# Graph attention layer: inverse sums and the shift's sign on POOL, output blocks finished in pairs

## What is computed

```python
h = relu(layernorm(x))                      # over the last axis, eps 1e-5
Wh = h @ W
f1, f2 = Wh @ a[:256, 0], Wh @ a[256:, 0]
e = f1[:, :, None] + f2[:, None, :]
e = where(e >= 0, e, 0.2 * e)
att = softmax(where(adj > 0, e, -9e15), axis=1)   # over i, for each column j
out = x + elu(einsum('bij,bjo->bio', att, Wh))
```

## Time and profile before

| | us |
|---|---|
| three runs | 1093.25, 1095.69, 1096.59; median 1095.69 |
| the profiled execution | 1092.74 |
| its span, from first to last instruction | 1091.0 |
| busy: PE, DVE, ACT, POOL | 972.8, 978.4, 958.3, 401.7 |
| first mask_scores begins | 61.9 |
| last mask_scores begins | 1049.8 |
| from one mask_scores to the next: middle of batch 7, middle of a batch 1 to 6 | 7.17 or 7.2, 7.3 to 8.7 |

### The profile page before, as it was taken

One profiled execution on the slowest core, in us unless ns is written; L12 is line 12 of the kernel. 1 busy time (PEld: TensorE's weight loads), 2 busy tenths in 40 slices (PEclk: granted clock), 3 DMA queues, 4 the chain that ended last, 5 costly groups with the idle time before them and its releaser, 6 DMA issues. The chain is left out here.

```text
span 1091.0 us, 24411 instructions
## 1 busy us (share of the span) xinstructions
PE 972.8 (89%) x8963; PEld 831.9 (76%) x8963; DVE 978.4 (90%) x1579; ACT 958.3 (88%) x1606; POOL 401.7 (37%) x317
## 2 busy tenths in 40 slices
PE   4667799899999999899998999999999999888987
PEld 3445688788878888787887888787887878777776
DVE  4379999999999999999999999999999999999973
ACT  3368999999999999998999999998999989988974
POOL 2313323334343433334343343334333343333334
PEclk9769999999999999999999999999999999999999
DMA  4366665666676676666766666766766566766614
GB/s 129 113 184 168 167 174 163 193 181 193 190 207 181 180 217 180 189 179 197 200 190 197 180 195 188 208 176 186 211 191 186 172 192 171 198 179 184 180 35 150
DMA packets 325654, 195.11 MB, mean 179 GB/s; under 512 B 9760, under 2 KB 321312, under 8 KB 325536
## 3 DMA queue, kind: packets, MB, share of 16 engines
q1 hardware_dynamic: 325536, 193.56, 62.2%
HBM read 176.69 MB, written 16.84 MB: 177 GB/s over the span
## 5 line engine op out<-in xcount | busy, mean ns | idle before, releaser
L689 POOL TENSOR_TENSOR direct<-prob,inv 128x1024 f16<-128x1024 f32 x128 | 242.6, 1895 | 590.7 <-DVE inv L605 585.2
L589 DVE CUSTOM_DVE_ANT_0 prob<-tp,f_row 128x2048 f32<-128x2048 bf16 x128 | 293.3, 2291 | 4.9 <-issue 4.4
L378 PE MATMUL acc<-v,direct 128*128 128x256 f16 x1024 | 280.2, 274 | 11.1 <-DVE direct L613 6.0
L360 PE MATMUL acc_st<-v,stored 128*128 128x256 f16 x992 | 270.2, 272 | 22.2 <-DVE z_st L629 21.6
L380 PE MATMUL acc<-v,direct 128*128 128x256 f16 x1024 | 279.9, 273 | 0.0
L382 PE MATMUL acc<-v,direct 128*128 128x256 f16 x1024 | 279.9, 273 | 0.0
L362 PE MATMUL acc_st<-v,stored 128*128 128x256 f16 x992 | 270.3, 272 | 0.0
L361 PE MATMUL acc_st<-v,stored 128*128 128x256 f16 x992 | 270.3, 272 | 0.0
L439 ACT ACTIVATE prob<-prob,shift 128x2048 f32<-128x2048 f32 x128 | 256.6, 2005 | 10.8 <-issue 0.4
L432 ACT ACTIVATE prob<-prob,f 128x2048 f32<-128x2048 f32 x128 | 255.6, 1997 | 0.0
L331 PEld LDWEIGHTS tp<-ident_b,neg 128*128 128x128 bf16 x2048 | 119.5, 98 | 94.1 <-issue 92.1
(11 more groups left out here) (71 smaller groups left out, 1222.4 us busy)
## 6 DMA issues: line engine op xcount, KB each, us to landing
raw<-in_adj SPq DMA_DIRECT2D x128, 1024.0 KB, 6.0
x_in<-in_x SPq DMA_DIRECT2D x128, 128.0 KB, 5.0
y<-in_x SPq DMA_DIRECT2D x128, 128.0 KB, 4.6
out<-y SPq DMA_DIRECT2D x128, 128.0 KB, 3.7
f_row<-f_scratch SPq DMA_DIRECT2D x32, 256.0 KB, 5.0
f_scratch<-f_t SPq DMA_DIRECT2D x128, 0.5 KB
w_cat<-in_W SPq DMA_DIRECT2D x1, 256.0 KB, 2.9
prob<-in_a SPq DMA_DIRECT2D x1, 256.0 KB, 3.7
```

Of the source, the lines that this page charges most:

```text
L360: nc.tensor.matmul(bank[:, 0:FO], p_st[:, 0, rows], v_c[:, 0, :], start=(c == 0), stop=False)
L378: nc.tensor.matmul(acc[:, m, :], p_d[:, 0, rows], v_c[:, 0, :], start=(j == 0 and m % 2 == 0), stop=False, skip_group_check=True)
L589: nc.vector.tensor_tensor_reduce(out=prob[:, c % 2, :], in0=tp_b, in1=f1_row[:, b % 2, :], scale=1.0, scalar=-3.0e38, op0=ALU.add, op1=ALU ...
L689: nc.gpsimd.tensor_tensor(direct[:, c % 2, 0, :], p[:, 0:HALF], k.to_broadcast([P, HALF]), ALU.mult).then_inc(hi_direct, 1)
```

## The change

POOL's `split_high(s)` first multiplies the sum by 2^-14 and raises it to the power -1 (column `minus_one`). ACT no longer negates the maximum: POOL's new `make_shift(s)` does, behind `split_high(s - 1)` and the additions of that step. DVE's `reciprocal` and `scale_inverse` are gone. Blocks are finished two at a time, 512 columns an instruction and 256 KB a transfer, in every second step. Buffers are changed to make room: one x buffer less, h_t single after the start. The diff, cut to its core:

```diff
-    RX = 7
+    RX = 6
-    RY = 8
-    RZ = 3
-    RE = 4
+    RY = 4
+    RZ = 4
+    RE = 2
...
-        h_t = sb("h_t", [P, 2, KC, P], F32)
+        h_t = sb("h_t", [P, KC, P], F32)
...
+        def h_buf(c):
+            return h_t_early if c < LEAD and c % 2 else h_t[:]
...
-        ORDER = {2: [0, 8], 3: [1], 4: [2], 5: [3, 9], 6: [4], 7: [5], 8: [6], 9: [7],
-                 10: [10], 11: [11], 12: [12], 13: [13], 14: [14], 15: [15]}
-        ORDER_LAST = {2 + q: [q, 8 + q] for q in range(8)}
+        ORDER = {2: [4], 3: [0], 5: [1], 7: [2], 9: [3], 11: [5], 13: [6], 15: [7]}
+        ORDER_LAST = {2: [4], 3: [0], 4: [5], 5: [1], 6: [6], 7: [2], 8: [7], 9: [3]}
...
-                if chunk(s + 25) and s + 25 >= RX:
-                    load_x(s + 25)
+                if chunk(s + 24) and s + 24 >= RX:
+                    load_x(s + 24)
...
+                wait(act, shift_s, c - R + 1)
                 nc.scalar.activation(most[:, c % R:c % R + 1], top[:, c % R:c % R + 1], ACT.Prelu, bias=f2, alpha=ALPHA
                                      ).then_inc(most_s, 1)
                 nc.scalar.activation(p, p, ACT.Prelu, bias=f2, alpha=ALPHA).then_inc(leaky, 1)
-                act.wait_ge(most_s, c + 1)
-                nc.scalar.activation(shift[:, c % R:c % R + 1], most[:, c % R:c % R + 1], ACT.Copy, scale=-1.0
-                                     ).then_inc(shift_s, 1)
                 act.wait_ge(leaky, c + 1)
                 act.wait_ge(shift_s, c + 1)
-                wait(act, recip_s, c - R + 1)
+                wait(act, total_s, c - R + 1)
...
-                if chunk(s):
-                    reciprocal(s)
-                    scale_inverse(s)
...
             def split_high(c):
                 p = prob[:, c % 2, :]
                 k = inv[:, c % R:c % R + 1]
+                t = small_total[:, c % R:c % R + 1]
+                pool.wait_ge(prob_ready, c + 1)
+                nc.gpsimd.tensor_scalar(t, total[:, c % R:c % R + 1], 2.0 ** -P_BITS, None, ALU.mult).then_inc(total_s, 1)
+                pool.wait_ge(total_s, c + 1)
+                wait(pool, lo_stored, c - R + 1)
+                nc.gpsimd.tensor_tensor(k, t, minus_one[:], ALU.pow).then_inc(inv_ready, 1)
                 pool.wait_ge(inv_ready, c + 1)
...
+            def make_shift(c):
+                pool.wait_ge(most_s, c + 1)
+                wait(pool, prob_ready, c - R + 1)
+                nc.gpsimd.tensor_scalar(shift[:, c % R:c % R + 1], most[:, c % R:c % R + 1], -1.0, None, ALU.mult
+                                        ).then_inc(shift_s, 1)
...
             for s in range(FIRST, END + 2):
                 if chunk(s - 1):
                     split_high(s - 1)
                 for k in finish(s - 2):
                     finish_add(k)
+                if chunk(s):
+                    make_shift(s)
```

More of the change, by code:

```diff
@@ L69, in graph_attention @@
         z_st = sb("z_st", [P, RZ, FO], F32)
-        elu = sb("elu", [P, RE, FO], F32)
+        elu = sb("elu", [P, RE, 2 * FO], F32)
         x_in = sb("x_in", [P, RX, F], F32)
-        y = sb("y", [P, RY, FO], F32)
+        y = sb("y", [P, RY, 2, FO], F32)
         xn = sb("xn", [P, 2, F], F32)
-        h_t = sb("h_t", [P, 2, KC, P], F32)
+        h_t = sb("h_t", [P, KC, P], F32)
         f12 = sb("f12", [P, 64 + RF], F32)
@@ L83, in graph_attention @@
         ones = prob[0:1, 0, 1024:1024 + P]
+        h_t_early = prob[:, 1, 1024:1024 + F].rearrange("p (k c) -> p k c", k=KC)
         w_nat = w_cat[:, :, 0:FO]
@@ L92, in graph_attention @@
         minus_half = sb("minus_half", [P, 4], F32)
+        minus_one = sb("minus_one", [P, 1], F32)
         top = sb("top", [P, R], F32)
@@ L96, in graph_attention @@
         total = sb("total", [P, R], F32)
-        inv_total = sb("inv_total", [P, R], F32)
+        small_total = sb("small_total", [P, R], F32)
         inv = sb("inv", [P, R], F32)
@@ L134, in graph_attention @@
         prob_ready = sem("prob_ready")
-        recip_s = sem("recip_s")
+        total_s = sem("total_s")
         inv_ready = sem("inv_ready")
@@ L226, in finish, with rows_of @@
             return finish_at.get(s, [])
-        def output_rows(k):
+        def rows_of(tensor, k):
             b, i = finishing[k]
-            r = (NB + i if i < NB else i - NB) * P
-            return b, slice(r, r + P)
+            r = (NB + 2 * i if i < 4 else 2 * (i - 4)) * P
+            return tensor[b, r:r + 2 * P, :].rearrange("(t p) f -> p t f", p=P)
         def h_prime(k):
             b, i = finishing[k]
-            return z_st[:, i % RZ, :] if i < NB else z_direct[:, i - NB, :]
+            z = z_st[:, 2 * i % RZ:2 * i % RZ + 2, :] if i < 4 else z_direct[:, 2 * (i - 4):2 * (i - 4) + 2, :]
+            return z.rearrange("p t o -> p (t o)")
         finish_index = {item: k for k, item in enumerate(finishing)}
@@ L287, in _ @@
                     wait(sp, y_out[k % RY], 16 * (k // RY))
-                    bo, rows = output_rows(k)
-                    sp.dma_start(y[:, k % RY, :], x[bo, rows, :]).then_inc(x_res_in[k % RY], 16)
+                    sp.dma_start(y[:, k % RY], rows_of(x, k)).then_inc(x_res_in[k % RY], 16)
                 for k in finish(s - 2):
                     sp.wait_ge(y_ready, k + 1)
-                    bo, rows = output_rows(k)
-                    sp.dma_start(out[bo, rows, :], y[:, k % RY, :]).then_inc(y_out[k % RY], 16)
+                    sp.dma_start(rows_of(out, k), y[:, k % RY]).then_inc(y_out[k % RY], 16)
                 if chunk(s + LEAD) and (s + LEAD) % 4 == 3:
@@ L296, in _ @@
             for i in range(RY):
-                sp.wait_ge(y_out[i], 16 * (B * C // RY))
+                sp.wait_ge(y_out[i], 16 * (len(finishing) // RY))
         @block.tensor
@@ L307, in make_wh @@
                 for k in range(KC):
-                    last = nc.tensor.matmul(wh_bank(c)[:, 0:FW], h_t[:, c % 2, k, :], w_cat[:, k, :],
+                    last = nc.tensor.matmul(wh_bank(c)[:, 0:FW], h_buf(c)[:, k, :], w_cat[:, k, :],
                                             start=(k == 0), stop=(k == KC - 1))
@@ L449, in make_h @@
                 act.wait_ge(xt_ready, c + 1)
-                wait(act, wh_ps, c - 1)
-                nc.scalar.activation(h_t[:, c % 2].rearrange("p k c -> p (k c)"), xt_bank(c)[:, 0:F], ACT.Relu
+                wait(act, wh_ps, c - 1 if c < LEAD else c)
+                nc.scalar.activation(h_buf(c).rearrange("p k c -> p (k c)"), xt_bank(c)[:, 0:F], ACT.Relu
                                      ).then_inc(ht_ready, 1)
@@ L466, in take_direct @@
                 act.wait_ge(direct_done, C * (b + 1))
-                wait(act, elu_ready, C * b)
+                wait(act, elu_ready, G * b)
                 m = slice(4 * h, 4 * h + 4)
@@ L475, in finish_relu @@
                 wait(act, y_ready, k - RE + 1)
-                if i < NB:
-                    act.wait_ge(z_stored, G * b + i + 1)
+                if i < 4:
+                    act.wait_ge(z_stored, G * b + 2 * i + 2)
                 else:
@@ L597, in split_v_low @@
                                                ).then_inc(v_ready, 1)
[L599 to L606, removed]
             def split_low(c):
@@ L626, in add_halves @@
                 if past >= 0:
-                    k_past = finish_index[(past // G, past % G)]
+                    k_past = finish_index[(past // G, past % G // 2)]
                     dve.wait_ge(elu_ready, k_past + 1)
@@ L674, in _ @@
             nc.gpsimd.memset(minus_half[:], -0.5)
+            nc.gpsimd.memset(minus_one[:], -1.0)
             nc.gpsimd.memset(ones, 1.0)
@@ L706, in finish_add @@
                 pool.wait_ge(x_res_in[k % RY], 16 * (k // RY + 1))
-                nc.gpsimd.tensor_tensor(y[:, k % RY, :], y[:, k % RY, :], elu[:, k % RE, :], ALU.add
-                                        ).then_inc(y_ready, 1)
+                pair = y[:, k % RY].rearrange("p t f -> p (t f)")
+                nc.gpsimd.tensor_tensor(pair, pair, elu[:, k % RE, :], ALU.add).then_inc(y_ready, 1)
             for s in range(FIRST, END + 2):
```

## The result

| | before | after |
|---|---|---|
| median of the timed runs, us | 1094.10 (7 runs) | 1098.97 (7 runs) |
| their range | 1092.33 to 1096.59 | 1097.75 to 1102.92 |
| the profiled execution, its span | 1092.74, 1091.0 | 1102.46, 1100.7 |

What follows compares the result with a forecast made beforehand. It took four rings of waits, not busy time, to bound the kernel. Start +1.2, batch 0 -2.8 and -1.0, first halves -2.4, the rest 0, sum to -5.0 us: from 1095.7 to 1090.7, range 1080 to 1109.

Steps and rivals of the forecast that it cites:

- The four rings: Repeating chains of waits said to bound four kinds of stretch: batch 0 (batch 7 alike), second halves, first halves, tail.
- second halves: Seven of sixteen steps, paced by PE's stored blocks at 8.12 us each; change expected 0.
- L605 behind a pair's addition: DVE's split_low (L613 before), shut out by POOL's addition in batch 7; forecast to take 2.1 us.
- The power's own time: POOL's one-column power in the inverse: 0.35 us fixed plus 0.17 for the column, 0.52, called P.
- the ring of 6.36 + P: Batch 0: ACT's ring, with P the power's time, 6.86 us against 7.17; nine steps save 2.8 us.
- two-step ring: Batch 7: a new ring closes over two steps, 14.4 us, 7.2 a step against 7.17; change 0.
- rival B: DVE's port lock delays every chunk's power, P = 1.99: +78 us, 1173, slower; chance 0.07.
- first halves: Batches 1 to 6, rounds of 7.65 us with ACT hardly idle: -0.4 us a batch, -2.4 in all.
- POOL's queue: make_shift, behind split_high and the addition, is ready 4.2 us after the last sum; Exp comes at 4.8, leaving 0.6.
- costed at nothing: First halves: seven single finishings become four pairs, one block more for about three fixed parts less; priced at zero.
- The start, +1.2: With six x buffers, x loads come later before the first sum: twice 0.6 us, +1.2.
- two thirds of 0.55, and 0.10: Chance of faster by over 0.3%, given as 0.48: two thirds of the main case (0.55) plus loosening rings (0.10).

Runs made afterwards that it cites:

- shift_first: The changed kernel with make_shift put ahead of the pair's addition on POOL; median 1094.14 us, ratio to before 1.0004.
- first_early: shift_first with DVE's finish_elu moved ahead of make_mask; median 1092.22 us, ratio to before 0.9989.
- shift_act: The changed kernel with the shift's sign made on ACT again; median 1093.60 us, ratio to before 0.9996.
- pairs_only: The changed kernel with the inverse back on DVE and the shift on ACT, leaving pairs and buffers; median 1101.43 us, ratio to before 1.0072.
- singles_act: The kernel before with only the inverse moved to POOL, blocks finished one at a time; median 1087.74 us, ratio to before 0.9935.
- singles: The kernel before with only inverse and shift moved to POOL, blocks finished one at a time; median 1088.99 us, ratio to before 0.9956.

## Why the prediction was wrong

**Right.** The four rings, and that busy time misleads: second halves did not move in any kernel but two (342.5 in shift_first and first_early). L605 behind a pair's addition: 2.08 against 2.1. The power's own time: 0.57 against 0.52. That was luck in part, for the fixed part of 0.35 came from a product of 1024 columns and an addition of 256, and a one-column product takes 0.21 in all; by the additions alone (0.73 for 256 columns, 1.27 for 512, where 1.12 was forecast) a column costs 2.1 ns and the fixed part is below 0.2. Batch 0: the ring of 6.36 + P with P = 0.57 gives 6.93, and 6.74 to 6.77 was measured; -4.9 against -3.8, of which 0.6 is the one long step of before. Batch 7: +0.4 against 0, and rightly as a two-step ring, whose steps alternate between 6.6 to 6.8 and 7.6 to 7.9 with an addition in every second. That rival B was not it: P is 0.57 or 0.58 in 116 of 128 steps, and 0.87 in the other 12.

**Wrong, first halves: +8.0 in place of -2.4.** Two steps failed.

The step "POOL's queue", by which make_shift is there 4.2 us after the last sum and 0.6 are left, took every instruction of POOL at its unhindered length. I had the exclusion in rows 6 and 7, and used it on the addition against split_low (L613, now L605) in batch 7, but did not follow it to the next instruction: L605 waits at the port when the addition ends, so whatever stands behind the addition waits for L605. Measured: 5.9 after the sum, Exp 0.74 late in every second step. shift_act and shift_first take away 8.0 and 6.7 us of first halves with that wait.

The step by which seven single finishings become four pairs, "costed at nothing", was wrong by 5.4 us (pairs_only, with the buffers that came with the pairs). I had named the alternation of heavy and light steps, and then booked it against a gain instead of pricing it.

Neither is the whole. By the ledger the parts are: inverse on POOL alone -3.6 (singles_act), the shift there too a further -2.5 as long as additions are single (singles), pairs with their buffers +5.4, and the shift behind a pair's addition +8.0 (after less shift_act). These parts are not a plain sum: the same shift gains with single additions and loses with pairs, and inverse and pairs together (shift_act) come to 0.0, not to +1.8.

**A rule set aside too early.** The Trainium skill (SBUF — State Buffer, "SBUF: two separate sides") names, beside instructions with two inputs from SBUF, DVE's two-port modes as holders of the lock. In the prediction it stood as something that no row showed. What it would mean for make_mask held: small_total and make_shift end 0.07 or 0.04 us after make_mask in the rows of first_early and singles. In which mode make_mask runs no row shows. In after, 55 of 128 small_total start under make_mask and take 0.59 on average, 0.4 more than alone.

**The start, +1.2:** not settled by the medians, as said; its profile value is inside what executions differ by. But the statistics wait 13.5 us in 10 places for x, 2.9 in one before, not twice 0.6.

**A sum:** two thirds of 0.55, and 0.10, are 0.47 and not 0.48.

## What to carry to other kernels

A short instruction on POOL can take as long as what DVE has at the shared port (here 0.22 became 1.19, and twice 2.28), so its place in POOL's queue is priced with DVE's order beside it: after each POOL instruction ask which DVE instruction is waiting, for in these traces it went first, and what stood next in POOL waited for all of that. Put what another engine waits for (here a one-column product of 0.2 us) on the engine that needs it: that gave the lowest time of the three places, both with pairs and with single additions. Ahead of the bulk work it gained with pairs (6.7 us in first halves) and lost with single additions (7.0), where the addition then ran up against split_low. And a change of several parts deserves a run of each part: here a gain of 0.65% was in it, hidden under the losses of the pairs and of the shift.

## What the runs showed that I had not expected

make_mask, one int32 tile in and bfloat16 out, 2048 columns in 1.22 us, shuts POOL out for all of that time; mask_scores, 2.28 us with one operand in PSUM, does not at all. An added 0.3 us in a chain of 7 cost 8.8 us in 1087, more than the two DVE instructions that the change took out had ever given back. The start to the first sum differs by 4.2 us between two executions of the same kernel (73.1 and 68.9), and by 5.4 between kernels that differ there only in who makes the shift.
